# Fp32 products of unsplit operands in the expert, projection, output and branch products of a two-layer kernel

## What must be computed

```python
# layer 0, attention (2 x 512 tokens of 256, 16 heads of 16, blocks of 32)
q, k, v = x @ Wq.T, x @ Wk.T, x @ Wv.T        # x: the normalised tokens; q, k rotated
gate = q . mean of k over each block           # the own block and the 3 best earlier ones are kept
p = softmax(where(kept and causal, q . k / 4, -1e30))
o = rmsnorm(p @ v) ;  attn = o @ Wo.T
# layer 0, experts (8 of 176 units, 2 per token, and a shared one of 352)
comb = top-2 of softmax(x @ gate_w)
g = silu(x @ w_gate[e]) * (x @ w_up[e])
moe = sum_e comb[t, e] * g @ w_down[e] + silu(x @ sw_gate) * (x @ sw_up) @ sw_down
x1 = x0 + (attention and experts joined)       # in the kernel: x0 + attn * silu(moe)
# layer 1, on the normalised x1
left  = gelu(x @ Wl + bl) ;  u = conv4(x @ Wr + br)
r, i  = sigmoid(u @ Wa + ba), sigmoid(u @ Wi + bi)
h_t   = a_t h_(t-1) + sqrt(1 - a_t^2) i_t u_t   # a = exp(-8 softplus(-lam) r)
mix   = (h * left) @ Wo + bo                    # then gated by an edit of the tokens
```

## Time and profile before

| | before |
|---|---|
| runs, median (lowest to highest) | 424.85 us (424.27 to 425.32) |
| profiled execution: first to last instruction (span) | 422.4 us |
| busy: PE / its weight loads / DVE / ACT / POOL | 348.9 / 240.3 / 300.3 / 170.7 / 172.9 us |
| DMA | 30.20 MB, mean 71 GB/s |
| mean granted clock of PE | 0.935 |

### The profile page before, as it was taken

The page is one execution under the profiler, slowest core; times in us unless marked ns, Lnnn a source line. Parts: engine busy times, 40 slices in busy tenths (PEclk is TensorE's granted clock), DMA queues, the critical chain, the costliest instruction groups (busy, mean ns, idle before and its releaser), DMA issues. The chain is left out here.

```text
span 422.4 us, 6057 instructions
## 1 busy us (share of the span) xinstructions
PE 348.9 (83%) x2028; PEld 240.3 (57%) x2028; DVE 300.3 (71%) x857; ACT 170.7 (40%) x305; POOL 172.9 (41%) x119
## 2 busy tenths in 40 slices
PE   0697767668779989999999999999682888996881
PEld 0586555546546657676665665656581776444641
DVE  3867489867997877894444764684668859758794
ACT  1422453551224323226444445544212475956610
POOL 5654283473444642554256526664536000000023
...
DMA packets 17009, 30.20 MB, mean 71 GB/s; under 512 B 3140, under 2 KB 12012, under 8 KB 16556
## 3 DMA queue, kind: packets, MB, share of 16 engines
...
## 5 line engine op out<-in xcount | busy, mean ns | idle before, releaser
L388 POOL TENSOR_TENSOR wl<-wr,wh 128x768 fp32r<-128x768 f32 x28 | 51.2, 1829 | 65.3 <-ACT wh L474 49.1
L530 ACT ACTIVATE PT<-bank 128x512 f32<-128x512 f32 (+1 forms) x88 | 44.3, 557 | 39.5 <-PE bank L952 39.4
L687 DVE TENSOR_REDUCE mx<-bank 128x1 f32<-128x384 f32 (+3 forms) x88 | 52.2, 635 | 7.2 <-PE bank L934 6.9
L149 PE MATMUL bank<-xh,wh 128*128 128x512 f32 x112 | 50.7, 452 | 4.0 <-DVE gb L812 1.4
L426 POOL TENSOR_TENSOR gl<-gb,gh 128x512 fp32r<-128x512 f32 x28 | 36.5, 1302 | 37.5 <-DVE gh L819 24.9
L151 PE MATMUL bank<-xh,wl 128*128 128x512 f32 x112 | 45.7, 408 | 0.0
L150 PE MATMUL bank<-xl,wh 128*128 128x512 f32 x112 | 45.5, 407 | 0.0
L933 PE MATMUL bank<-KS,QS 112*128 112x128 bf16 (+3 forms) x128 | 32.9, 310 | 12.5 <-DVE mx L687 6.8
L1213 POOL TENSOR_TENSOR left<-xn,x 128x256 f32<-128x256 f32 x8 | 7.0, 898 | 85.1 <-DVE xn L1440 85.1
L149 PE MATMUL bank<-wh,gh 128*128 128x256 f32 x112 | 36.9, 329 | 0.5 <-POOL gl L426 0.5
L537 ACT ACTIVATE th<-bank 128x512 f32<-128x512 f32 x28 | 16.7, 597 | 45.9 <-PE bank L151 45.8
...
## 6 DMA issues: line engine op xcount, KB each, us to landing
...
```

The source lines that it names most:

```text
L149: pe.matmul(out, l_hi, r_hi, start=start, stop=False, skip_group_check=skip)
L388: pool.tensor_tensor(wl[:, s % 3, :, :], wr[:, s % 2, :, :], wh[:, s % 3, :, :].bitcast(F32), ALU.subtract).then_inc(wl_ready, 1)
L530: act.activation(PT[:, k % 8, 0:n], bank[k % 2][:, 0:n], ACT.Exp, scale=float(DH) ** -0.5).then_inc(P_ready, 1)
L687: dve.tensor_reduce(mx[:, b * TB + i, heads[0]:heads[-1] + 1], bank[k % 2][:, 0:len(heads) * n].rearrange("p (h n) -> p h n", n=n), AX.X, ...
```

## The change

The products of `project`, `gate_product`, `up_product`, `down`, the output product and `branch_in` take unsplit fp32 operands, so `split_matmul`, all roundings and all subtractions of operands go. Since `gb` no longer has to be split, it becomes the moving operand of `down` and the chunk's weights the stationary one, two products of 512 tokens instead of four pairs of 256 columns. The result then has features on the partitions (`yT`), goes through tanh and SiLU in that form and is transposed on PE at the end (`transpose_gate`), and ACT copies it out (`gate_rows`). The chunks have four buffers, filled as soon as the step that read one is done. POOL weighs the gated tile in every routed step, so ACT copies the weights in each of them, and ACT's tanh waits for the gated tile of the step before. In layer 1 ACT and DVE copy one half each of `xT`, where ACT rounded all and DVE subtracted and then copied.

On PE, in step 13 before: the up product and the first half of down. `xh`, `xl` are the split tokens, `wh`, `wl` the split chunk, `gh`, `gl` the split gated tile; A_read counts row maxima that DVE has taken.

```diff
...
 def pool_weighs(s):
 
-    return A_SLOT // SLOTS <= s < DVE_STEP and s % CH < ECH
+    return s % CH < ECH
+
+
+ON_BANKS = [0, 1, 2, 5]
+Y_BANKS = [[6, 7], [3, 4]]
+S_BANKS = [6, 7, 3, 4]
...
-def split_matmul(pe, out, l_hi, l_lo, r_hi, r_lo, start, stop, skip=False):
-
-    pe.matmul(out, l_hi, r_hi, start=start, stop=False, skip_group_check=skip)
-    pe.matmul(out, l_hi, r_lo, start=False, stop=False, skip_group_check=skip)
-    return pe.matmul(out, l_lo, r_hi, start=False, stop=stop, skip_group_check=skip)
...
-            pool.wait_ge(wph_ready, 1)
-            pool.tensor_tensor(wp_l[:, :, :], wp[:, :, :], wp_h[:, :, :].bitcast(F32), ALU.subtract).then_inc(wpl_ready, 1)
-
-            def split_chunk(s):
-                pool.wait_ge(wh_ready, s + 1)
-                if s >= 3:
-                    pool.wait_ge(down_done, s - 2)
-                pool.tensor_tensor(wl[:, s % 3, :, :], wr[:, s % 2, :, :], wh[:, s % 3, :, :].bitcast(F32),
-                                   ALU.subtract).then_inc(wl_ready, 1)
...
                 if pool_weighs(s):
                     done = sum(pool_weighs(r) for r in range(s + 1))
                     pool.wait_ge(uv_ready, done)
                     pool.wait_ge(weights_read, done)
-                    pool.wait_ge(gh_ready, s)
-                    pool.wait_ge(gl_ready, s)
-                    pool.tensor_tensor(gb[:, :], uv[:, :], th[:, :], ALU.mult).then_inc(g_ready, 1)
-                pool.wait_ge(gh_ready, s + 1)
-                if s >= 2:
-                    pool.wait_ge(down_done, s - 1)
-                pool.tensor_tensor(gl[:, s % 2, :], gb[:, :], gh[:, s % 2, :].bitcast(F32),
-                                   ALU.subtract).then_inc(gl_ready, 1)
-                if s == WO_STEP:
-                    pool.wait_ge(woh_ready, 1)
-                    pool.tensor_tensor(wo_l[:, :, :], wo[:, :, :], wo_h[:, :, :].bitcast(F32),
-                                       ALU.subtract).then_inc(wol_ready, 1)
+                    if s >= 2:
+                        pool.wait_ge(down_done, s - 1)
+                    pool.tensor_tensor(gb[:, s % 2, :], uv[:, :], th[:, :], ALU.mult).then_inc(g_ready, 1)
...
             def load_chunk(s):
-                if s >= 2:
-                    act.wait_ge(wh_ready, s - 1)
-                    act.wait_ge(wl_ready, s - 1)
-                act.dma_start(wr[:, s % 2, :, :], a["w_chunks"][s % CH]).then_inc(w_in[s % 2], 16)
+                if s >= WBUF:
+                    act.wait_ge(down_done, s - WBUF + 1)
+                act.dma_start(wr[:, s % WBUF, :, :], a["w_chunks"][s % CH]).then_inc(w_in[s % WBUF], 16)
...
+            def gate_rows(n):
+
+                for k in range(2):
+                    act.wait_ge(yTT_ready, 2 * n + k + 1)
+                    act.copy(y[:, n * TB + 2 * k:n * TB + 2 * k + 2, :],
+                             bank[Y_BANKS[n][k]][:, :].rearrange("p (t d) -> p t d", d=D)).then_inc(y_ready, 1)
...
                 act.wait_ge(G_ready, s + 1)
                 if s >= 1:
                     act.wait_ge(G_read, s)
+                    act.wait_ge(g_ready, s)
...
-                act.copy(xh[:, n % 2, (n // 2) * S:(n // 2 + 1) * S], bank[n][:, :]).then_inc(onh_ready, 1)
+                act.copy(xT[:, n % 2, (n // 2) * S:(n // 2 + 1) * S], bank[ON_BANKS[n]][:, :]).then_inc(onT_copied, 1)
+            gate_rows(1)
...
-                half = y[:, n * TB:(n + 1) * TB, :]
-                link(dve.scalar_tensor_tensor(out=half, in0=yth[:, n * TB:(n + 1) * TB, :], scalar=1.0, in1=half,
-                                              op0=ALU.add, op1=ALU.mult))
+                dve.scalar_tensor_tensor(out=yT[:, n, :, :], in0=yth[:, n, :, :], scalar=1.0, in1=yT[:, n, :, :],
+                                         op0=ALU.add, op1=ALU.mult).then_inc(yT_ready, 1)
...
-                elif c < ECH:
-                    link(dve.scalar_tensor_tensor(out=uv[:, :], in0=s2[:, :], scalar=0.5, in1=bank[4][:, :],
-                                                  op0=ALU.mult, op1=ALU.mult))
-                    dve.tensor_tensor(gb[:, :], uv[:, :], bank[5][:, :], ALU.mult).then_inc(g_ready, 1)
                 else:
-                    dve.scalar_tensor_tensor(out=gb[:, :], in0=s2[:, :], scalar=0.5, in1=bank[4][:, :],
+                    if s >= 2:
+                        dve.wait_ge(down_done, s - 1)
+                    dve.scalar_tensor_tensor(out=gb[:, s % 2, :], in0=s2[:, :], scalar=0.5, in1=bank[4][:, :],
                                              op0=ALU.mult, op1=ALU.mult).then_inc(g_ready, 1)
-                if s >= DVE_STEP:
-                    dve.wait_ge(g_ready, s + 1)
-                    dve.wait_ge(down_done, s - 1)
-                    dve.tensor_copy(gh[:, s % 2, :], gb[:, :]).then_inc(gh_ready, 1)
                 for q in range(s * SLOTS + 1, (s + 1) * SLOTS):
...
-                w = s % 3
-                pe.wait_ge(wl_ready, s + 1)
+                w = s % WBUF
+                pe.wait_ge(w_in[w], 16 * (s // WBUF + 1))
                 if s >= 1:
                     pe.wait_ge(G_read, s)
                 for k in range(KD):
-                    ins = split_matmul(pe, bank[3][:, :], wh[:, w, k, 0:P], wl[:, w, k, 0:P],
-                                       xh[:, k, part], xl[:, k, part], k == 0, k == KD - 1)
+                    ins = pe.matmul(bank[3][:, :], wr[:, w, k, 0:P], xT[:, k, part], start=(k == 0), stop=(k == KD - 1))
...
-                c, w = s % CH, s % 3
-                pe.wait_ge(gl_ready, s + 1)
+                c = s % CH
+                pe.wait_ge(g_ready, s + 1)
                 if c == 0 and s:
                     pe.wait_ge(y_read, 2)
-                for o in range(2):
-                    ins = split_matmul(pe, bank[6 + k][:, o * D:(o + 1) * D],
-                                       gh[:, s % 2, tokens(2 * k + o)], gl[:, s % 2, tokens(2 * k + o)],
-                                       wh[:, w, 2, :], wl[:, w, 2, :], c == 0 and o == 0, c == CH - 1, skip=True)
+                ins = pe.matmul(bank[6 + k][:, :], wr[:, s % WBUF, 2, tokens(k)], gb[:, s % 2, :],
+                                start=(c == 0), stop=(c == CH - 1))
                 if k:
                     ins.then_inc(down_done, 1)
+
+            def transpose_gate(n):
+
+                pe.wait_ge(yT_ready, n + 1)
+                if n == 0:
+                    pe.wait_ge(y_read, 2 * HALVES)
+                for k in range(2):
+                    for i in (2 * k, 2 * k + 1):
+                        for c in range(KD):
+                            ins = pe.transpose(bank[Y_BANKS[n][k]][:, (i % 2 * KD + c) * P:(i % 2 * KD + c + 1) * P],
+                                               yT[:, n, c, tokens(i)], ident[:, :])
+                    ins.then_inc(yTT_ready, 1)
...
+            transpose_gate(0)
             for n in range(2 * B):
                 b, c = n // 2, n % 2
                 pe.wait_ge(on_ready, (b + 1) * NG)
                 for i in range(TB):
-                    ins = pe.transpose(bank[n][:, i * P:(i + 1) * P], xn[:, b * TB + i, c * P:(c + 1) * P], ident[:, :])
+                    ins = pe.transpose(bank[ON_BANKS[n]][:, i * P:(i + 1) * P], xn[:, b * TB + i, c * P:(c + 1) * P],
+                                       ident[:, :])
                 ins.then_inc(onT_ready, 1)
-            pe.wait_ge(woh_ready, 1)
-            pe.wait_ge(wol_ready, 1)
+            transpose_gate(1)
+            pe.wait_ge(sem_wo, 16)
             for n in range(T // 2):
-                pe.wait_ge(onl_ready, 2 * (2 * n // TB + 1))
+                pe.wait_ge(onT_copied, 2 * (2 * n // TB + 1))
+                pe.wait_ge(y_ready, 2)
                 if n >= 2:
-                    pe.wait_ge(gated_ready, n - 1)
+                    pe.wait_ge(y_ready, 4)
                 for t in (2 * n, 2 * n + 1):
                     for c in range(KD):
-                        ins = split_matmul(pe, bank[4 + n % 2][:, t % 2 * D:(t % 2 + 1) * D],
-                                           xh[:, c, tokens(t)], xl[:, c, tokens(t)],
-                                           wo_h[:, c, :], wo_l[:, c, :], c == 0, c == KD - 1, skip=True)
+                        ins = pe.matmul(bank[S_BANKS[n]][:, t % 2 * D:(t % 2 + 1) * D], xT[:, c, tokens(t)],
+                                        wo[:, c, :], start=(c == 0), stop=(c == KD - 1), skip_group_check=True)
                 ins.then_inc(s_ready, 1)
 
 
...
-            act.wait_ge(w_in["lr"], 16)
-            act.copy(w_lr_h[:, :, :], w_lr).then_inc(wh_ready, 1)
-            for n in range(2 * B):
-                b, c = n // 2, n % 2
-                act.wait_ge(xT_ready, n + 1)
-                act.copy(xh[:, c, b * S:(b + 1) * S], bank[n][:, :]).then_inc(xh_ready, 1)
+            for b in range(B):
+                act.wait_ge(xT_ready, 2 * b + 1)
+                act.copy(xT[:, 0, b * S:(b + 1) * S], bank[2 * b][:, :]).then_inc(xT_copied, 1)
...
```

(5 more changed lines are left out.)

148 lines of the change are left out of this document (41 added, 107 removed).

## The result

| | before | after | forecast |
|---|---|---|---|
| runs, median (lowest to highest) | 425.09 us (424.27 to 425.98, 4 runs) | 439.06 us (436.16 to 441.73, 4 runs) | 445.0 (437 to 452) |
| ratio to before | | 1.0328, 95% interval 1.0265 to 1.039 | 1.047 |
| profiled execution (span) | 422.4 us | 436.6 us | 442.7 |
| busy: PE / DVE / ACT / POOL | 348.9 / 300.3 / 170.7 / 172.9 us | 373.0 / 260.1 / 153.0 / 94.4 us | |
| mean granted clock of PE | 0.935 | 0.966 | |

In a second series of six runs the changed kernel took 440.47 us (439.11 to 442.95), ratio 1.0393 (1.0343 to 1.0443). Its ten runs lie between 436.16 and 442.95 us, those of the kernel before in the second series between 421.47 and 427.66.

What follows compares the result with a forecast made beforehand. PE was taken as the bound in steps 12 to 26; terms 1.1 + 0.7 + 0.5 + 5.4 + 9.9 + 2.4 + 0.3 = +20.3 us on 424.85 gave near 445 us, own range 440 to 450, 8 in 10: 437 to 452.

Steps and rivals of the forecast that it cites:

- PE's clock stays up: Rival: longer products leave fewer pauses, half clock falls three times less and the start warms up at once: -6, 439 us; chance 0.14.
- signs that I had named for being wrong: Unsplit products under 0.70 us apart, PE waiting for the gated tile in steps 16 to 26, or steps 8 to 15 unchanged.
- Pace: Expert products: 0.86 us unsplit against 0.70 for three reduced; +0.9 us a step, +9.9 us in steps 16 to 26.
- the busy column: Rival: judged by record lengths without overlap, gate and up save 1.9 us a step, time near 400 us; chance 0.03.
- four passes: Expert products: with a full four, a product 0.93 us, a step +1.4, the sum some 9 us higher; not taken.
- Steps 8 to 15: Eight steps at +0.9, 7.2 us, less 1.8 of PE's 6.8 us of waits for maxima: +5.4 us.
- Cost 0, with 4 us of cover: Expert steps: POOL's weighting of the gated tile ahead of ACT's next tanh was to cost nothing.
- The rival had put it at 12: Rival: the hand-over to POOL becomes the bound, 1.5 us for each of eight roots, 457 us; chance 0.09.
- I let that cost 2.2 again: Start, projection: PE's half clock was to cost 2.2 us as before, possibly 0.2 to 3.6.
- The pile-ups: Both starts: DVE's 3.5 us normalisation beside POOL's subtraction goes; projection 2.75 us earlier, branch products 1.9 us earlier.
- The tail's +2.4: End of layer 0: added transposes, longer output product and more time at half clock, +2.4 us (+0.5 to +3.5).
- Half of the 2.1 is taken as a chance: Layer 1, products with w_f: 5.84 us, 3.7 at full clock; half of the difference counted as gain, -1 us.

Runs made afterwards that it cites:

- experiment 2: Changed kernel with each of the six products of a step replaced by three rounded matmuls on a constant tile (experts' results not computed): 423.77 us, ratio to before 0.998.
- experiment 3: Changed kernel where PE's up product and value-sum transposes wait for the readers of banks 4 and 5, not for POOL's weighted tile: 438.17 us.
- experiment 4: Changed kernel with DVE weighing the gated tile again in routed steps 0 to 4 and 16 to 24, as before the change: 440.11 us.
- experiment 10: Changed kernel with the first eight transposes of the gated tile moved behind those of the heads: 444.55 us in the first series, 443.70 us in the second.
- experiment 6: Kernel before, with both subtractions of weights moved from POOL to DVE, behind the normalisations: 421.33 us, ratio 0.9907.
- experiment 8: Kernel before with the projection weights' subtraction on DVE, and layer 1 of the changed kernel: 421.27 us, ratio 0.9916.
- experiment 7: Layer 0 of the kernel before with layer 1 of the changed kernel: 422.10 us, ratio 0.9938.
- experiment 9: The kernel of experiment 3 with eight chunk buffers, chunks 2 to 7 loaded during the projection: 434.56 us, ratio 1.0236.

## Why the prediction was right, and where it was not

The sign and the range of 437 to 452 held, and the mechanism on which the sign rested, PE's pace. The forecast overshot by 6 us: 439.06 lies just below its own range (440 to 450), and on the figure of the rival "PE's clock stays up" (439), to which I had given 0.14. The rival's mechanism was there: the mean clock rose from 0.935 to 0.966, which is some 30 us of the span at half clock for 55. That its figure was met is luck all the same. Its own terms, 3 x 1.7 and the 2.2 of the start, make -7.3 and not -6, and the measured 439 is a sum of misses that in part cancel. Against the forecast the six stretches are off by -1.2, -1.7, +2.4, -3.6, -3.6 and +1.6 us. One of the signs that I had named for being wrong came true as well: PE waited for the gated tile in steps 16 to 26, 2.4 us in 4 waits, and a step took 10.75 us where I had 10.5 and no idle time.

**Pace.** Right, and more than the whole of the loss (experiment 2: 16.7 us, where the change lost 14.0 and 15.7 in the two series). An fp32 product takes 0.86 us in a queue and three reduced ones 0.70; the busy column, by which the change should have gained 20 us and more, misled as said. Without the hand-over steps 16 to 26 cost 115.24 for 105.92, +0.85 a step where I took 0.9. The Trainium skill's four passes (FP8 and Floating Point Precision, TensorE Precision Notes) would have made a step 1.4 us longer, if a pass is a reduced product of 0.233 us. That "if" was the mistake in my working: a bf16 matmul of 512 columns takes 210.39 - 210.17 = 0.22 us in the rows of step 17, and four of those are 0.88, near the 0.86 measured. The trace agrees with the page, and it is the reduced product that costs a little more than a pass.

**Steps 8 to 15.** "Less the part of PE's waits for maxima that a slower PE no longer has, 1.8 of the 6.8 us": the waits fell by 3.6, but 1.5 of that lie ahead of step 8. Within steps 8 to 15 PE's idle time fell from 3.30 (63.41 less 60.11) to 0.97 us, by 2.3. The greater part of the miss is the other term: PE's busy time rose by 5.98 us, 0.75 a step where I had 0.9. 5.98 - 2.33 is the +3.65 measured. Why the pace costs less there than in steps 16 to 26 is open.

**Hand-over.** "Cost 0, with 4 us of cover" failed. I had looked at the order of tanh and at POOL's roots, and not at two things: ACT's copy of the weights stands behind exponentials, and the semaphore of the tile also guards bank 5, for PE's transposes. Price 3.0 us (experiments 3 and 4). The rival had put it at 12.

**Start.** "I let that cost 2.2 again" failed. The projection started at 14.76 (15.42 forecast) and at full clock; the 16 transposes in front of it came in one piece:

```profile
11.29 3.63 PE L779 MATMUL bank<-ident,x 128*128 128x128 f32 x16 [11.29 <-DVE x L537]
14.76 1.88 PE L789 MATMUL bank<-wp,xT 128*128 128x512 f32 x4
16.48 1.05 PE L793 MATMUL bank<-wp,xT 128*128 128x264 f32 x4
17.37 1.88 PE L789 MATMUL bank<-wp,xT 128*128 128x512 f32 x4
```

That one piece of transposes is enough for the full clock is not shown. In the profile of experiment 10, with the same start, the first four records of the projection took 2.74 us, for 1.88:

```profile
15.11 2.74 PE L789 MATMUL bank<-wp,xT 128*128 128x512 f32 x4
```

And experiments 6 and 8, whose layer 0 is the same and whose projections both start at 16.72 behind 16 transposes, had records of 0.63 and of 0.39 us there. The cost of the clock at this start is thus some 0 to 0.9 us, by the execution, and not 2.2.

A tile takes 17.37 - 14.76 = 2.61 us, for 2.60 forecast. Tanh of step 0 came 1.3 us earlier, that of step 5 3.8. Then the transfer took it all back. SyncE's queue in after:

```profile
57.76 1.26 SPq L329 DMA_DIRECT2D QS<-parts_dram  x3
59.06 7.10 SPq L316 DMA_DIRECT2D parts_dram<-x  x6
76.29 2.63 SPq L332 DMA_DIRECT2D KS<-parts_dram  x6
78.96 1.20 SPq L305 DMA_DIRECT2D bias_dram<-biasT  x2
92.62 0.31 SPq L308 DMA_DIRECT2D QS<-bias_dram  x1
```

And in before:

```profile
60.22 3.81 SPq L330 DMA_DIRECT2D parts_dram<-x  x6
76.20 2.62 SPq L346 DMA_DIRECT2D KS<-parts_dram  x6
83.07 1.20 SPq L319 DMA_DIRECT2D bias_dram<-biasT  x2
92.05 0.31 SPq L322 DMA_DIRECT2D QS<-bias_dram  x1
```

The bias goes out 4.1 us earlier and comes back 0.6 us later: by these rows it comes back behind the stacked keys, which start at the same time in both, 16 us ahead of its return (15.8 to 17.5 us in five profiles, whenever the bias went out). They wait for the parts, and the parts are what the start moves: they went out 1.2 us earlier in after and took 1.3 us longer.

**The ends.** The pile-ups went as forecast: the branch products start 11.2 us behind the output product, for 13.55, 2.35 us gained where I had 1.9. The tail's +2.4 was wrong by the clock: PE's pause is now 1.5 us, filled by transposes, and all is at full clock (7.07 us for the output product, 7.68 before). "Half of the 2.1 is taken as a chance" in layer 1: it was all of it, in every profile of the changed layer 1 (4.56 or 4.57 us for the products with w_f, 5.84 before). Both ends together came out 7.2 us better than forecast, which is more than the 6 by which the whole overshot. By my estimate from the rows some 4.3 us of it are the clock: 2.2 in the output product, 1.1 in the products with w_f, 1.0 in the branch products of the first batch. The last of these is chance, as experiments 4, 7 and 9 show. Against that, the last stretch lost 1.6 us, which nothing in the change explains: its first 24 products with `w_o` took 8.40 us for 6.83, at half clock for longer. They took 7.33 in the second profile of the same kernel, 7.01 in experiment 3 and 8.45 in experiment 7: this is chance, too.

**The port.** That POOL's weighting would hold up DVE's two-input instructions (the Trainium skill, SBUF — State Buffer, Who interferes with whom) happened where I had not looked for it: in step 20 DVE's scaling of a head took 1.52 us from 242.55, beside POOL's tile at 242.53; in the tail, with POOL idle, the same line took 0.43. It is no new cost: before, the same instruction took up to 1.39 us, beside POOL's subtraction for `gl`. PE had cover for it.
